# Second attention hop and mean layer of a graph network: own rows added on TensorE, another order of steps, 12 fillers for 48, and joined row transfers

## What is computed

```python
agg = segment_sum(edge_weight[:, None] * x[edge_col], edge_row)
out = concatenate([agg, x], axis=1) @ W.T          # layer norm, gamma, beta, relu
x = _layernorm(x + relu(...))
```

```python
def agg(x):
    e = leaky(sum((concatenate([x[head], x[tail]]) @ fc_w.T + fc_b) * rel_e))
    w = exp(e - segment_max(e, head)) / denom[head]
    return segment_sum(x[tail] * w[:, None], head) + x
for _ in range(n_hops):
    x = agg(x)
    x = x / maximum(norm(x), 1e-12)
    res = res + x
```

## Time and profile before

| | us |
|---|---|
| median of 3 runs | 6968.55 (6963.94 to 6973.09) |
| the profiled execution | 6984.61 |
| its span, first to last instruction | 6982.7 |
| mean layer (TensorE's first to last instruction, 710 to 1660) | 950 |
| first hop (l2a, about 3958 to 4895) | 937 |
| second hop (l2b, about 4895 to 5925) | 1030 |
| interaction layer | 1057 |

### The profile page before, as it was taken

One profiled execution on the slowest core, in us unless ns is written; L12 is line 12 of the kernel. 1 busy time (PEld: TensorE's weight loads), 2 busy tenths in 40 slices (PEclk: granted clock), 3 DMA queues, 4 the chain that ended last, 5 costly groups with the idle time before them and its releaser, 6 DMA issues. The chain is left out here.

```text
span 6982.7 us, 169103 instructions
## 1 busy us (share of the span) xinstructions
PE 6298.9 (90%) x37102; PEld 5098.3 (73%) x37103; DVE 5285.4 (76%) x18168; ACT 4280.0 (61%) x14748; POOL 3904.1 (56%) x3592
## 2 busy tenths in 40 slices
PE   5676899997789998989999899999899998999999
PEld 2222788886688887769999788888566666888887
DVE  9887888887655654247777677777688887899998
ACT  0000899995214443238888677777588787677777
POOL 6677777775736666754444444444444444444443
PEclk9555999998879999999999899999899999999999
DMA  1200666666656666667777666665577676444443
GB/s 40 6 2 8 182 193 193 194 194 192 182 154 192 199 197 186 198 186 222 222 222 222 178 185 187 186 187 173 176 221 216 205 221 184 123 126 127 128 127 118
DMA packets 1224976, 1161.36 MB, mean 166 GB/s; under 512 B 314483, under 2 KB 1152523, under 8 KB 1224094
## 3 DMA queue, kind: packets, MB, share of 16 engines
q1 hardware_dynamic: 1067230, 943.02, 43.9%
q0 software_dynamic: 157632, 217.06, 13.3%
HBM read 946.93 MB, written 395.69 MB: 192 GB/s over the span
## 5 line engine op out<-in xcount | busy, mean ns | idle before, releaser
L215 POOL DMA_INDIRECT l_gathered<-x,by_dst_meta x384 | 433.6, 1129 | 547.7 <-PE l_ps_a L1571 485.8
L1836 POOL DMA_INDIRECT l2b_gathered<-z,by_src_meta x408 | 431.1, 1057 | 534.9 <-PE l2b_ps_g L2079 419.6
L1836 POOL DMA_INDIRECT l2a_gathered<-x,by_src_meta x408 | 431.1, 1057 | 453.8 <-PE l2a_ps_g L2079 338.1
L215 POOL DMA_INDIRECT l1b_gathered<-messages,by_dst_meta x384 | 395.3, 1029 | 437.8 <-PE l1b_ps_b L1434 376.8
L215 POOL DMA_INDIRECT l1a_gathered<-messages,by_dst_meta x384 | 432.1, 1125 | 206.7 <-PE l1a_ps_b L1434 141.7
L700 PE MATMUL l2b_ps_x<-zero_row,ones_b 128*128 128x392 bf16 x2912 | 510.1, 330 | 0.0
L215 POOL DMA_INDIRECT l_gathered<-in_x,by_src_meta x384 | 417.7, 1088 | 130.7 <-issue 113.9
L889 PE MATMUL l_ps_b<-l_w,l_x_t 128*128 128x256 f32 x1592 | 416.2, 384 | 38.8 <-DMA l_x_t<-in_x_turned 37.8
L865 ACT ACT_TABLE_LOAD x1 | 1.3, 1283 | 702.6 <-PEq L129 702.6
L1432 PE MATMUL l1b_ps_b<-root,l1b_x_t 128*128 128x256 f32 x1600 | 425.8, 389 | 0.0
L1432 PE MATMUL l1a_ps_b<-root,l1a_x_t 128*128 128x256 f32 x1584 | 415.6, 385 | 3.8 <-DVE l1a_hot L670 1.6
(11 more groups left out here) (402 smaller groups left out, 20682.5 us busy)
## 6 DMA issues: line engine op xcount, KB each, us to landing
x<-l1b_result SPq DMA_DIRECT2D x400, 152.0 KB, 3.0
z<-l2a_result SPq DMA_DIRECT2D x400, 152.0 KB
l2a_x<-x SPq DMA_DIRECT2D x53, 1024.0 KB
l2b_x<-z SPq DMA_DIRECT2D x53, 1024.0 KB
l1b_x<-h SPq DMA_DIRECT2D x408, 128.0 KB
l1b_res<-x SPq DMA_DIRECT2D x408, 128.0 KB
l2b_res<-x SPq DMA_DIRECT2D x51, 1024.0 KB
l_x_t<-in_x_turned SPq DMA_DIRECT2D x406, 128.0 KB
```

Of the source, the lines that this page charges most:

```text
L215: pool.indirect_dma_start(gathered[:, slot, 0:D], None, source[0:count, :], bass.IndirectOffsetOnAxis(ap=rows, axis=0), bounds_check=limit ...
L1836: pool.indirect_dma_start(gathered[:, k, :], None, x_in[0:N_NODES, :], bass.IndirectOffsetOnAxis(ap=rows, axis=0), bounds_check=limit, oob ...
```

## The change

**Second hop.** The own rows are no longer added on DVE. The hop's sum is not divided by the denominator either: since the result is divided by its own norm, agg / denom + x and agg + denom x x give the same after that division. The sum of x weighted by the denominator is built by TensorE: for each item a second matmul adds `diagonal` x own rows into the same `ps_g` tile, where `diagonal` holds each node's share of that item on its diagonal (`own_share`: the share from ACT, plus 1 where the node's maximum stands at the floor). The steps `divide` and `add_self` leave DVE's list, `weigh_own` comes in (share, a 128x1024 product for the eight diagonals, the denominator's scan, the guard `least`). `add_residual` and the squares on ACT read `agg`, which now holds 16 items. DVE's order is new: `add_residual` and `centre` first, `weigh_own` next, and the two halves of `add_up` stand on either side of `find_nodes`; `maximum` follows the second half at once. On TensorE 12 fillers stand where 48 stood, and a second register load (`find_own`). SP's `load_x` waits for `x_added`.

**Mean layer.** The rows and the turned rows of a tile lie side by side in one input (`x_both`), and one transfer of 256 KB brings both, into 16 buffers instead of 8. The first 16 loads no longer wait for the zeroing of buffers; each later one waits for `summed`. The loop bodies cover 8 pairs instead of 4.

```diff
-        x, gathered, agg_t, x_t, products, ... = (ph.sb(k, [P, RING, D], F32) ...)
+        both = ph.sb("both", [P, HOP, 2 * D], F32)
+        x, x_t = both[:, :, 0:D], both[:, :, D:2 * D]
...
-                later = ((x_t, x_in_t, s["in_xt"], s["b_done"], 6),)
-                move_tiles(sp, graph, s, x, x_in, result, x_out, later, lead=2)
+                for half in range(2):
+                    rows = rows_of(load_regs, LOAD, half * RING)
+                    for k in range(RING):
+                        load(rows[k], half * RING + k)
...
+                        for k in range(RING):
+                            sp.wait_ge(s["summed"], first + (k + 1))
+                            load(next_rows[k], half * RING + k)
+                            sp.wait_ge(s["out_ready"], first + (k + 1))
+                            sp.dma_start(x_out[bass.ds(rows[k], P), :], result[:, k, :]).then_inc(s["stored"][k], 16)
...
+                def weigh_own(o):
+                    pass_wait(dve, s, s["shrunk"], o.number + 1)
+                    pass_wait(dve, s, s["chance"], o.item + OCT)
+                    dve.scalar_tensor_tensor(own_share[:, o.both], below[:, o.half, :], -FLOOR, share[:, o.both], ALU.is_ge, ALU.add)\
+                        .then_inc(s["own_share"], 1)
+                    o.wait(dve, s["own_share"])
+                    if o.after(1):
+                        pass_wait(dve, s, s["x_added"], o.item)
+                    dve.tensor_tensor(diagonal[:], c.ident[:].unsqueeze(1).broadcast_to([P, OCT, P]),
+                                      own_share[:, o.both].unsqueeze(2).broadcast_to([P, OCT, P]), ALU.mult)\
+                        .then_inc(s["diagonal"], 1)
...
-                    steps = [(add_residual, 0), (find_slots, 1), (scores, 2), (divide, 1), (part(add_up, 0), 1), (centre, 0), (part(add_up, 1), 1),
-                             (part(add_self, 0), 1), (part(add_self, 1), 1), (have_variance, 0), (maximum, 2), (have_square, 1),
-                             (find_nodes, 3), (lambda o: inv2.square(dve, o), 0), (lambda o: inv2.weigh(dve, o), 0),
+                    steps = [(add_residual, 0), (centre, 0), (weigh_own, 1), (scores, 2), (part(add_up, 0), 1), (find_slots, 1),
+                             (find_nodes, 3), (part(add_up, 1), 1), (have_variance, 0), (maximum, 2), (have_square, 1),
+                             (lambda o: inv2.square(dve, o), 0), (lambda o: inv2.weigh(dve, o), 0),
...
                 def aggregate(o, n):
+                    if last_hop:
+                        at = slots_of(pe, own_regs)
+                        if n == 0:
+                            o.wait(pe, s["diagonal"])
+                            pe.wait_ge(in_x[o.half], (o.lap + 1) * 16)
...
+                        if last_hop:
+                            pe.matmul(ps_g[:, k % OCT, :], diagonal[:, k % OCT, :],
+                                      x[:, bass.ds(at[k % OCT] + o.base, 1), :].rearrange("p k d -> p (k d)"), start=False, stop=True)\
+                                .then_inc(s["x_added"], 1)
...
-                    steps = [(find_slots, 3)] + [(part(aggregate, n), 1) for n in range(4)] + [
-                        (spread, 2), (part(fill, 48), 2), (part(turn_chances, 0), 2), (part(fill, 4), 2),
+                    steps = [(part(aggregate, n), 1) for n in range(4)] + [
+                        (spread, 2), (find_own, 2), (find_slots, 3), (part(fill, 12), 2), (part(turn_chances, 0), 2), (part(fill, 4), 2),
                         (part(turn_chances, 1), 2), (look_up, 3), (part(fill, 4), 2)]
```

More of the change, by code:

```diff
@@ L694, in wait_items, with __init__, each_wide @@
         eng.wait_ge(sem, self.item + 2)
+class WidePair(Pair):
+    def __init__(self, group, n):
+        super().__init__(group * 2, n)
+        self.wide = 2 * n % HOP
+        self.wide_lap = group + n // RING
+    def each_wide(self):
+        return [(self.item + q, self.slot + q, self.wide + q) for q in range(2)]
 def keep_busy(pe, c, spare, n):
@@ L714, in run_pairs, with run_wide_pairs @@
                 step(Pair(g, n + ahead))
+def run_wide_pairs(eng, graph, steps):
+    hops = load_hops(eng, graph)
+    for n in range(-max(ahead for _, ahead in steps), 0):
+        for step, ahead in steps:
+            if n + ahead >= 0:
+                step(WidePair(0, n + ahead))
+    with eng.Fori(0, hops) as g:
+        for n in range(RING):
+            for step, ahead in steps:
+                step(WidePair(g, n + ahead))
 class Norm:
@@ L784, in mean_layer @@
             s[k] = ph.sem(k)
-        s["in_xt"] = [ph.sem(f"in_xt{k}") for k in range(RING)]
+        in_both = s["in_x"] + [ph.sem(f"in_x{k}") for k in range(RING, HOP)]
         s_records, s_sources = ([ph.pool_dma_sem(f"{n}{k}") for k in range(2)] for n in ("records", "sources"))
@@ L790, in _, with rows_of, load @@
             def _(sp):
-                later = ((x_t, x_in_t, s["in_xt"], s["b_done"], 6),)
-                move_tiles(sp, graph, s, x, x_in, result, x_out, later, lead=2)
+                store_regs, load_regs = ([sp.alloc_register(f"l0_{n}_{k}") for k in range(RING)] for n in ("store", "load"))
+                def rows_of(regs, field, first_item):
+                    sp.load(regs, graph.table[0:1, field, bass.ds(first_item, RING)])
+                    return [sp.snap(r, min_val=0, max_val=ALL_ROWS - P) for r in regs]
+                def load(row, slot):
+                    sp.dma_start(both[:, slot, :], x_both[bass.ds(row, P), :]).then_inc(in_both[slot], 16)
+                for half in range(2):
+                    rows = rows_of(load_regs, LOAD, half * RING)
+                    for k in range(RING):
+                        load(rows[k], half * RING + k)
+                sp.wait_ge(s["zeroed"], 2)
+                for slot in range(RING):
+                    sp.dma_start(x_out[ROWS + slot * P:ROWS + (slot + 1) * P, :], result[:, slot, :])\
+                        .then_inc(s["stored"][slot], 16)
+                hops = load_hops(sp, graph)
+                with sp.Fori(0, hops) as g:
+                    for half in range(2):
+                        first = g * HOP + half * RING
+                        rows = rows_of(store_regs, STORE, first)
+                        next_rows = rows_of(load_regs, LOAD, first + HOP)
+                        for k in range(RING):
[3 more added lines that the diff above has]
+                            sp.dma_start(x_out[bass.ds(rows[k], P), :], result[:, k, :]).then_inc(s["stored"][k], 16)
+                for slot in range(RING):
+                    sp.wait_ge(s["stored"][slot], (hops * 2 + 1) * 16)
+                    sp.sem_inc(s["passed"], 1)
+                for slot in range(HOP):
+                    sp.wait_ge(in_both[slot], (hops + 1) * 16)
+                    sp.sem_inc(s["passed"], 1)
             @block.gpsimd
@@ L1764, in load_x @@
                     if octet.after(2):
-                        sp.wait_ge(s["y"], octet.item - OCT)
+                        sp.wait_ge(s["x_added"] if last_hop else s["y"], octet.item - OCT)
                         sp.sem_inc(s["passed"], 1)
@@ L2132, in project, with find_own @@
                     last.then_inc(s["projected"], 1)
-                pe_regs = [pe.alloc_register(f"{name}_pe_slot_{k}") for k in range(OCT)]
+                pe_regs, own_regs = ([pe.alloc_register(f"{name}_pe_{n}_{k}") for k in range(OCT)] for n in ("slot", "own"))
+                def find_own(o):
+                    load_slots(pe, own_regs, o)
                 def find_slots(o):
```

92 lines of the change are left out of this document (58 added, 34 removed).

## The result

The change made the kernel slower: 7162.08 us median (7159.50 to 7165.94, 4 runs) against 6966.24 us of before (6962.54 to 6973.09, 4 runs), ratio 1.0277 with a 95% interval of 1.0263 to 1.0290. The direction was forecast, the size was not: 196 us in place of 98.

A forecast was written before the change was run, and what follows sets the result against it. DVE was taken to set the hop's 19.18 us octet, POOL to fill the mean layer. 6984.61 + 103 (hop, 21.2 us an octet) - 5 (mean layer) = 7083 us profiled, 7067 median; range 6938 to 7145.

The forecast's parts named there:

- the new loop at full clock: Second hop, maximum to maximum through chances, fillers, sums and second half of `add_up`: 18.56 us, 0.62 less than 19.18.
- VectorE late with diagonal and second half: Second hop: lateness of VectorE's diagonals and second half of `add_up` had no term in the forecast sum.
- the clock's falls: Second hop, behind TensorE's wait for the chances: a fall in 8 of 10 octets, 3.3 us each, 2.6 us per octet.
- The way over DVE: Second hop, maximum to sums: residual starts 3.9 us behind maximum, diagonals end at about 8.7, against 9.26 for TensorE's way.
- the half microsecond by which the masks hold up the second half of `add_up`: Second hop: 0.5 us, counted only in the 14.7 us from residual to maximum of the rival with the residual's late load.
- the 2.6 to 3.1 worked out: Second hop: TensorE waits 2.6 to 3.1 us per octet between 12 fillers and the turned chances.
- the signs named for a right forecast: Hop: clock 0.80 to 0.92, waits of 2.6 us or more, `below` at 21 us intervals, busy DVE about 14.5 us an octet.
- falls in every octet and stays low longer: Rival, second hop: clock falls each octet for longer, 22.8 us an octet, +178 us, 7146 us; chance 14%.
- The late residual load: Rival, second hop: clock holds, the residual's load becomes the bound, 19.8 us an octet, 6994 us; chance 10%.
- The mean layer: Joined transfers and more buffers cost nothing while POOL is full; -5 us with the earlier start, ends -38 to +10.
- the ring: Second hop: chain of steps and waits that comes back to its start each octet and sets its length.

The follow-up runs named there:

- e6: Changed kernel with 28 fillers, own rows weighed ahead of the residual and masks at the end of VectorE's list: 6945.39 us, ratio 0.9963 to the kernel before.
- e14: e6 with the mean layer of the kernel before: 6942.00 us, ratio 0.9959 to the kernel before, 18.55 us per octet.
- e1: Changed kernel with 28 fillers in place of 12 ahead of the turned chances: 7079.87 us, ratio 1.0155 to the kernel before, 20.92 us per octet.
- e12: e6 with 12 fillers instead of 28, on a chip of the usual kind: 7046.91 us, ratio 1.0107 to the kernel before, 20.44 us per octet.
- e7: Changed kernel with 28 fillers and only the slots and node masks moved ahead of the first half of the sums: 7084.38 us, ratio 1.0156 to before.
- e13: e6 without the last 4 fillers between look-up and sums, on a usual chip: 6928.03 us, ratio 0.9945 to the kernel before, 18.35 us per octet.
- e3: Kernel before with 12 fillers for 48 and nothing else changed: 7154.39 us, ratio 1.0261 to before, 22.42 us per octet.
- e10: e6 without the last 4 fillers, on the chip where everything was slower: 7978.84 us, ratio 0.9984 to the kernel before there.

## Why the prediction missed in size

The median moved by 196 us. The profiled executions differ by 178, of which the hop is 184; these can be split, with each part measured by a run:

| part | forecast, us per octet | measured | by |
|---|---|---|---|
| the new loop at full clock, VectorE never late | -0.62 | -0.63 | e6, e14: 18.55 |
| VectorE late with diagonal and second half | 0 | +2.37 | e1 against e6; change against e12: 2.35 |
| the clock's falls | +2.6 | +1.87 | change against e1; e12 against e6: 1.89 |
| sum, times 51 | +103 | +184 | |

- **The step that failed** is the sentence "The way over DVE (maximum, residual, diagonals, then sums) is about half a us shorter". In the sum that way cost nothing; with the masks' part (next point) it was 2.37 us per octet, more than the clock's 1.87. The sentence took the start of the residual behind the maximum, 5.2 us in the earlier trace rows, and subtracted the two masks, to get 3.9. But the masks had covered the wait for ScalarE's logarithm and exponential (the first guess of the inverse root). Before, the step that needs it follows the last of the masks without a pause:

```profile
5388.23 0.35 DVE L1889 TENSOR_TENSOR l2b_kind<-by_src_meta,iota 128x192 f32<-128x192 f32 x1
5388.49 0.15 DVE L1622 TENSOR_TENSOR l2b_inv_a<-l2b_inv_y 128x8 f32<-128x8 f32 x1
```

With the masks gone it waits 0.73 us (5548.02 above), and in every second octet VectorE pauses some 0.8 us longer at the loop's end, put down to issue. So the residual starts 4.47 us behind the maximum in one octet of the changed kernel (5549.60 - 5545.13) and 5.26 in one with 28 fillers (5514.99 - 5509.73). The diagonal starts 8.43 us behind the maximum in one octet with 28 fillers (5498.08 - 5489.65) and 9.38 in the next (5519.11 - 5509.73), takes 1.22, and ends at 9.7 and 10.6 in place of 8.7. TensorE starts the sums about half a microsecond behind its end, 10.1 and 11.2 us behind the maximum; in e6, where it does not wait for the diagonal, it is 9.2 (5523.83 - 5514.59). That is late by 1.4 us on average.
- The prediction named the half microsecond by which the masks hold up the second half of `add_up`, but only in a rival, not in the sum; it was 0.65. It is also why TensorE waits 3.3 us for the chances in the changed kernel and 2.8 in e12, within the 2.6 to 3.1 worked out. The rest of the 2.37 us, some 0.3, fits the falls of the clock that e1 still has (9 of 51 octets).
- **The clock** was right in place and kind: waits ahead of the turned chances, a fall behind nearly each. In 46 of the 48 octets of the changed kernel whose second half of the turned chances the trace has whole, its matmuls run at the lower clock (1.0 to 1.1 us for four in place of 0.66). The term of 2.6 us was 0.8 falls of 3.3; measured are 1.87, with a fall in nearly every octet. One reason can be read: time that TensorE loses in the fall is partly time in which it would have waited for the diagonal, 35.9 us in 29 waits with 28 fillers and 5.1 in 6 in the changed kernel (5200 to 5800). In e12, which has no such waits, 38 of 49 octets fall, and a fall costs 2.6 us on average. The Trainium skill (TensorE: Matmul & The Clock Gate, HAM oscillation — how this bites in real kernels) describes this restart at the lower clock, and the windows agree. Its advice on gaps would have allowed the 1.79 us of e7 and the 2.79 us of e12, behind which the traces show slow octets; the measurement decides. Of the signs named for a right forecast the clock (0.82), the waits and busy DVE came true, and the distance of 21 us between two `below` did not.
- **The rival "falls in every octet and stays low longer"** gave 22.8 us per octet and 7146 us, nearly what came. It was right for the wrong reason: with its price of 4.2 us per fall the kernels with 28 fillers would have had to be faster than before. Of each octet only 1.87 us are the clock's. That the time came so near it is luck.
- The late residual load did not come up in the changed kernel; its octet was long enough, as the text had it. Nor did it in e6 at 18.55 us, where VectorE starts the residual later; the rival's own case, octets of 19.8 us in the change's order, did not occur in any run. The mean layer did what was forecast: POOL full, no waits for `l_both`, no gain that the medians show.

## What to carry to other kernels

When an edit moves a step out of a stretch, don't subtract its duration from the stretch: find which wait it had covered, and price the other engine's way to the same point as carefully as the one that you believe to be the bound. After such an edit run one version in which the suspected cost is taken away (here more fillers); that it wins back half says that there are two causes. What is still open is whether the own rows on TensorE pay at all: the kernel before with 48 fillers and nothing but its masks moved was not run, so the 0.4% of e6 are the whole change with its repaired order. And let steps without a deadline (here masks for three octets ahead) stand where an engine waits anyway, not between two steps of the ring: the order of the list was worth 134 us of median here at the same work.

## Unexpected on the hardware

- Equal waits had unequal outcomes: with the same waits for the diagonal of 0.7 and 1.8 us in turn the mean clock was 0.98 in one kernel (e1) and 0.93 in another (e7). With waits of 2.8 us (e12), 11 of 49 octets kept their time, and a fall lasted some 3 us or, as in the window of 5122.50, 10 us in which TensorE was busy throughout. And the clock fell in e13 where TensorE had hardly waited.
- But the outcomes are not thrown at random. In the changed kernel, from 5522 on, the octets take about 22.8, 23.7, 23.6 and 22.2 us, six times running; in e3 octets of 23.6, 23.4, 23.6, 23.7, 22.5 and 19.7 us come four times running; in e12 18.6, 19.7 and 23.1 keep coming back, with 21.5 and 19.7 put in between. So the same wait meets the clock differently from octet to octet, in a fixed turn. What sets the turn was not tested; the mean over many octets is what can be carried over.
- One chip ran the kernel before in 7984 us where the others of the experiments took 6970 to 6973. In the second hop of e10 VectorE's maximum waited up to 6.6 us, and pauses of up to 1.1 us put down to issue stood ahead of TensorE's fillers, which wait for nothing. What is slow there was not tested.
